# The convolution's 49 products stand at other LSTM steps of a turn

## The reference, cut to what matters

```python
# layer 2, ffn: one step after the other, t = 0..1023
i_t = sigmoid(xi_t + h @ V_i);  g_t = tanh(xg_t + h @ V_c);  o_t = sigmoid(xo_t + h @ V_o)
c_new = h * c + i_t * g_t
h_new = o_t * tanh(c_new)
# layer 3, conv: 7 x 7, each channel by itself, then relu
y = conv_general_dilated(x, kern, (1, 1), 'SAME', feature_group_count=c)
y = relu(y)
```

## Time and profile before

| | us |
|---|---|
| median of 3 runs | 3159.26 (3159.11 to 3162.25) |
| the profiled execution: its span, first to last instruction | 3157.1 |
| PE busy | 2771.7 (88%) |
| DVE busy | 1953.5 (62%) |
| ACT busy | 1668.0 (53%) |
| POOL busy | 874.9 (28%) |
| the convolution's matmuls (line 1152), 2646 records | 452.7 busy |

### The profile page before, as it was taken

The page is one execution under the profiler, slowest core; times in us unless marked ns, Lnnn a source line. Parts: engine busy times, 40 slices in busy tenths (PEclk is TensorE's granted clock), DMA queues, the critical chain, the costliest instruction groups (busy, mean ns, idle before and its releaser), DMA issues. The chain is left out here.

```text
span 3157.1 us, 64810 instructions
## 1 busy us (share of the span) xinstructions
PE 2771.7 (88%) x22240; PEld 2231.2 (71%) x22240; DVE 1953.5 (62%) x8535; ACT 1668.0 (53%) x5755; POOL 874.9 (28%) x1499
## 2 busy tenths in 40 slices
PE   4477888899999999999999999999998787887667
PEld 3366666678888788888888888788777564555556
DVE  5466666676667677777766667677754324555454
ACT  1245555566666666666665666666654423443333
POOL 2233222233233333323333333333311000000444
PEclk8677766688888888888888888888886688998888
DMA  2000000000000100000000000000000001000000
GB/s 100 14 17 18 18 19 19 19 19 19 21 21 20 32 19 19 19 19 19 19 19 19 21 21 25 27 19 19 19 17 9 3 2 28 1 1 1 8 10 11
DMA packets 54039, 59.12 MB, mean 19 GB/s; under 512 B 26576, under 2 KB 45136, under 8 KB 53328
## 3 DMA queue, kind: packets, MB, share of 16 engines
q1 hardware_dynamic: 53712, 54.99, 6.0%
HBM read 42.37 MB, written 4.19 MB: 15 GB/s over the span
## 5 line engine op out<-in xcount | busy, mean ns | idle before, releaser
L1072 DVE TENSOR_TENSOR_SCAN r_c<-r_wk 64x24 f32<-64x24 f32 x1024 | 244.3, 239 | 490.4 <-ACT r_wk L1058 486.5
L1058 ACT ACTIVATE r_wk<-psL 64x16 f32<-64x16 f32 x1024 | 189.1, 185 | 678.1 <-PE psL L1048 659.9
L1152 PE MATMUL psL<-img,dg 128*128 128x128 f32 x2646 | 452.7, 314 | 0.0
L1047 PEld LDWEIGHTS psL<-r_h,lv 128*64 128x64 f32 x2048 | 235.6, 162 | 291.1 <-DVE r_h L1077 162.9
L1047 PE MATMUL psL<-r_h,lv 128*64 128x8 f32 x2048 | 324.6, 231 | 80.6 <-DVE r_h L1077 74.8
L1152 PEld LDWEIGHTS psL<-img,dg 128*128 128x128 f32 x2646 | 378.4, 215 | 11.8 <-issue 3.9
L1049 PE MATMUL psL<-r_h,lv 128*64 128x8 f32 x2048 | 326.4, 232 | 0.0
L1048 PE MATMUL psL<-r_h,lv 128*64 128x8 f32 x2048 | 304.7, 222 | 0.0
L1077 DVE SCALAR_TENSOR_TENSOR r_h<-r_wk,r_tc 64x8 f32<-64x8 f32 x1024 | 196.3, 192 | 115.0 <-ACT r_tc L1063 101.5
L1063 ACT ACTIVATE r_tc<-r_c 64x8 f32<-64x8 f32 x1024 | 215.5, 210 | 83.8 <-DVE r_c L1072 37.7
L1048 PEld LDWEIGHTS psL<-r_h,lv 128*64 128x64 f32 x2048 | 252.7, 171 | 0.0
(11 more groups left out here) (376 smaller groups left out, 6558.8 us busy)
## 6 DMA issues: line engine op xcount, KB each, us to landing
accb<-acc_in SPq DMA_DIRECT2D x64, 512.0 KB, 4.3
a_xy<-a_E SPq DMA_DIRECT2D x512, 16.0 KB, 1.8
W<-pack_in SPq DMA_DIRECT2D x1, 3165.0 KB, 13.7
x6d<-X SPq DMA_DIRECT2D x64, 32.0 KB
out_x<-X SPq DMA_DIRECT2D x32, 64.0 KB, 1.6
X<-x_in SPq DMA_DIRECT2D x1, 1856.0 KB, 17.7
W<-pack_in SPq DMA_DIRECT2D x1, 1331.0 KB, 5.8
X<-x_in SPq DMA_DIRECT2D x1, 192.0 KB
```

Source lines behind the costliest of these rows:

```text
L1047: nc.tensor.matmul(psL[0:64, par, c:c + LB], lv[:, 0], h, start=False, stop=False, skip_group_check=True)
L1058: nc.scalar.activation(o, psL[0:64, par, c:c + 2 * LB].rearrange("p (g b) -> p g b", b=LB), ACT.Tanh).then_inc(sem("r_gi"), 1)
L1072: v.tensor_tensor_scan(r_c3[:, t % 2, :], r_wk[:, 0:24], r_wk[:, 30:54], 0.0, ALU.mult, ALU.add).then_inc(sem("r_c"), 1)
L1152: last = nc.tensor.matmul(o, dg[:, ky * KT + kx], rows[:, :, ky, kx:kx + IMG], start=(n == 0), stop=(n == KT * KT - 1))
```

## The change

The row of due times of the convolution's 28 pieces on PE is another one, and the row of its one piece on ACT, the eviction, goes from slot 27 to 27.5. No instruction is added, removed or altered; each engine's program holds the same instructions in another order. In the turns without a convolution row nothing changes.

```diff
     mybir.EngineType.Activation: (
         None,
-        (27,),
+        (27.5,),
...
     mybir.EngineType.PE: (
         None,
-        (0, 0, 0, 0.5, 0.5, 7, 8.5, 8.5, 9.5, 10, 11, 11, 12, 13.5, 15.5, 16, 16.5, 16.5, 16.5, 18, 18, 18, 18, 18.5, 18.5, 19.5, 20, 21),
+        (0, 0.5, 1, 1.5, 9, 9, 16, 16, 18, 18.5, 19, 19.5, 20, 20, 20.5, 21, 21, 21.5, 22, 22, 22.5, 23, 23.5, 24, 24.5, 25, 25.5, 26.5),
```

## The result

The changed kernel takes 3262.7 us (median of 4 runs, 3256.4 to 3265.2), the kernel before 3160.8 (4 runs, 3159.1 to 3167.8). The ratio is 1.0315, 95% interval 1.0293 to 1.0336: slower, as forecast, but by 102 us where 47 were forecast, and 0.7 us above the top of the range. The profiled span grew from 3157.1 to 3254.6 us, by 97.5; PE's busy time only by 39 us, to 2810.8.

The account below looks back on a forecast made before the run. The prediction saw an apparent PE bound hiding two clock states, full and half. Terms summed to +1.35 us a turn, 1.76 with late rises, times 27 = +47, giving 3206 us; range 3138 to 3262.

Parts of the forecast that it names:

- late rises: PE's clock comes back only in step 4; expected in about one turn in ten, at +5.45 us a turn.
- term 2: Steps 10 to 12, eight products less: -0.65 us a turn, not 1.9, since ACT's table load and gelu stand ahead.
- term 3: Step 14, two products less: -0.5 us a turn, no wait taking their place.
- term 4: Step 17, four products less: 0, since they filled a wait for DVE's state update.
- term 5: Step 18, six products less: -0.95 us a turn, not 1.4, bound by ACT's copy and tanh.
- term 8: Steps 28 to 31, unchanged in work, the clock now falling within them: -0.3 us a turn.
- term 10: Steps 0 and 1, four products less: nothing gained, +0.2 us a turn, entered and left at half clock.
- term 9: ACT's eviction moved behind step 28's tanh pair: 0, covered by DVE; without that cover 0.28 us a turn, 8 in all.
- Term 11: Step 2, two products more and the clock rising only near its end: 4.45 us against 2.25, +2.2 a turn.
- rival A: Clock rises in step 1 as before, so the kernel is faster: -0.55 us a turn, 3144 us; chance 0.28.
- Term 7: Steps 22 to 27, 21 products more, now at full clock: 11.1 us against 9.67, +1.45 a turn.
- rival E: Clock falls in mid turn, as where steps 10 to 12 ran at 0.69: up to +3.5 us a turn; chance 0.05.

Follow-up runs that it names:

- Experiment 3: Kernel before with only ACT's eviction of the finished row moved from slot 27 to 27.5; 3157.5 us, ratio 0.9989.
- experiment 1: Changed kernel with a turn's first ten products back at steps 0 and 1 (6 and 4); 3214.5 us, ratio 1.0165.
- experiment 2: Kernel before with only the thin start: 2, 4, 2 products in steps 0 to 2, two more in step 7; 3225.3 us, ratio 1.0204.
- experiment 4: Changed kernel with four unread matmuls added in step 0, ahead of each turn's first product; 3232.1 us, ratio 1.0228.
- experiment 5: Changed kernel with the products of steps 22 to 25 joined in the first slot of their step; 3280.5 us, ratio 1.0358.
- experiment 12: Changed kernel's thin start and eviction, with products kept in steps 9, 10, 11, 14 and 16 and fewer in 19 to 27; 3245.0 us, ratio 1.0271.
- experiment 9: Changed kernel with the old due times for the products of turns 27 to 31; 3231.6 us, ratio 1.0223.

## Why the prediction was right in sign and short by half

The two turns 14 against each other give +2.67 us, for a forecast of +1.35 (medians over turns 6 to 25: 75.16 against 72.74, +2.4; the turn of the earlier trace rows was one of the shorter ones). That the measured time is within a microsecond of the range is luck: the top of the range was made of late rises, and this kernel has none.

Terms 1 to 6, 8 and 10 held within 0.1 us each: -0.13, -0.63, -0.54, 0, -0.94, +0.05, -0.27 and +0.20. Step 17 takes 2.58 us with four products or none, step 18 takes 2.16, steps 10 to 12 give 0.63 for eight products and not 1.9; that the covers were named, and not only the products counted, made these right. Experiment 3 shows term 9 on the kernel before: its interval ends at +3 us, below the 8 us of a turn without that cover.

Term 11, the clock in step 2, was the right mechanism and nearly the right size: +2.42 in turn 14, +2.55 in the median, for +2.2. The rise comes near the end of step 2 (0.56 is 0.88 of the 4.67 us at half clock, 4.1 us; forecast 4.0). Experiments 1, 2 and 4 show it from three sides; rival A needed the clock back a microsecond into the step. The late rise that was put at one turn in ten did not occur in this kernel; it does in experiments 2, 5 and 12.

Term 7 was mis-sized: +2.51 for +1.45. The step-by-step forecast was 2.01, 2.25, 2.21, 1.77, 1.35 and 1.53; measured 2.41, 2.38, 2.10, 2.16, 1.46 and 1.67. The clock is full throughout, as said, so the fault is in PE's need. Joining the split products returns 0.28 in each of steps 22 and 25, 0.6 in all: 0.24 us a product came from step 18, where products stand in one run, and a run broken by small matmuls costs more. Whether it is the change of weights or the place at the end of the step that costs it, the experiment does not separate. Of the other 0.5 us the traces place a part: even in one run, the four products of step 23 hold PE from 1404.72 to 1405.81, 0.27 us each, 0.1 more for the four than by the forecast's price, and the same is seen in step 25 of the joined kernel. Step 24 was forecast 0.1 too high. The rest, 0.1 each in steps 26 and 27, stayed unexplained.

The greater failure is in two other steps of the prediction. "The last five of the 27 turns have lost one stage or more; I count them alike": they cost 25.9 us in four of them (27 to 30), 6.5 a turn, and experiment 9 shows that it is the due times in those turns that cost it. The rows of turn 27 show a fall in mid turn and late products that cost 2.9 us in steps 22 to 27. Why these turns suffer more than a full one is argued and not shown: what fills steps 3 to 16 in an ordinary turn is partly gone there, and products made up more of what was left. And rival E, the fall in mid turn, got a chance of 0.05 with "step 9 keeps its three products" against it. The prediction had the right row, steps 10 to 12 without a product at 0.69, and did not give it its weight; nor did it see that a fall there runs on into steps 13 to 21 and costs 9 us and not 3.5. It came in two of the 22 turns, which take 9.6 and 11.4 us more than before. So: 50 + 21 + 26 + 1, where the forecast had 1.35 x 27 = 36 and 11 for the late rises.

The rule of the Trainium skill that the prediction weighed (TensorE: Matmul & The Clock Gate, Terms: throttled time times one minus the clock ratio) does not order these kernels. The half-clock stretches that begin in turns 5 to 26 sum to 423.3 us in the changed kernel and to 467.6 in the kernel before. By that rule the clock alone should give back 22 us there; the turns take 70.7 us more. What half clock costs goes by place. In steps 0 and 1 it costs 0.2 us of 5.87. Steps 28 to 31 take 9.49 us at 0.50 and 8.81 at 0.73 (experiment 4), 0.7 us for 4.7 us more at half clock. But 4.1 us of it in step 2 cost 1.9 (4.67 against 2.77 in experiment 4), near the rule's half, and 23.9 us of it in steps 13 to 21 cost 9.4.

Open: what decides in which turn a middle fall comes (5 and 21 in one execution of this order, 15 and 26 in another, experiment 9), when the turns beside it hold the same work; and why joining the products, which shortens the work, goes with a later rise in half of the turns. Both may lie in how one fall of the clock sets the place of the next, which no run here takes apart.

## What to carry to other kernels

Where an engine's clock follows its own activity, as PE's does here (unread matmuls in step 0 brought the rise forward out of step 2), find the stretches that are cheap at half clock (the engine waits for others there) and the dense ones that are not; work may be moved as long as the cheap stretch still holds the whole of the slow time, and work just ahead of a dense stretch can be worth more than its own length (here four matmuls a turn gave back 30 us). Price a moved instruction by a row in which it stands next to what it will stand next to, since a run of equal ones is the cheapest case. A loop's ramp-down needs its own sum: what costs 2.4 us when all stages run cost 10 us in each of the first two turns in which some were gone. And one profile is one execution: count rare events such as the falls in mid turn in more than one before a difference is put down to the change.

## What the runs showed of the hardware

Adding work made the kernel faster, twice: four unread matmuls a turn took 30 us off the changed kernel (3232.1 for 3262.7), two more of them took it to 3221.7, a step only just clear of its interval. Taking 0.6 us of PE time out of each turn did not make it faster (3280.5, by ratio 14 us slower). The changed kernel's undisturbed turns lie within 75.0 to 75.8 us through 20 turns, while those of the joined one, with less work, swing between 74.4 and 78.5. Where the clock falls in mid turn differs between two executions of the same order. And one half-clock stretch of 23.9 us in a dense place costs as much as the change costs in four ordinary turns.
